# Softmax sums of a causal attention transposed and inverted once per query on VectorE, in a four-layer kernel with a hand-written order

## The reference

```python
x = L0(x)   # attention over 1024 tokens, query and key of width 32, x + gamma * out
x = L1(x)   # group norm, attention of width 256, output projection, x + out
x = L2(x)   # layer norms, 8 heads of width 32, causal, one key and value head, feed-forward
x = L3(x)   # as L1 with its own weights

# the part of L2 that the change touches
sim  = jnp.einsum('bhid,bjd->bhij', q, k)          # k, v shared by the 8 heads
sim  = jnp.where(causal, neg, sim)
attn = jax.nn.softmax(sim, axis=-1)                 # = exp(..) / sum of exp(..)
out  = jnp.einsum('bhij,bjd->bhid', attn, v)
out  = out.transpose(0, 2, 1, 3).reshape(b, n, INNER) @ wo
```

## Time and profile before

| | us |
|---|---|
| median of 3 runs | 1383.55 (1383.23 to 1387.08) |
| the profiled execution | 1385.56 |
| its span, first to last instruction | 1383.8 |
| PE busy | 1292.8 (93%) |
| DVE busy | 866.0 (63%) |
| ACT busy | 593.9 (43%) |
| POOL busy | 93.9 (7%) |
| mean granted clock of TensorE | 0.981 of full speed |

### The profile page before, as it was taken

How to read it: one execution, slowest core, us unless ns; L and a number is a source line. 1 busy time by engine, 2 the same in 40 slices (tenths; PEclk the granted TensorE clock), 3 DMA queues, 4 the chain that set the end, 5 groups by cost and what they waited for, 6 DMA issues and landing times.

```text
span 1383.8 us, 21791 instructions
## 1 busy us (share of the span) xinstructions
PE 1292.8 (93%) x8800; PEld 1011.3 (73%) x8800; DVE 866.0 (63%) x1854; ACT 593.9 (43%) x973; POOL 93.9 (7%) x134
## 2 busy tenths in 40 slices
PE   6979999889999999999999999999999999999898
PEld 5868777666678767677788667777787767768786
DVE  3634456787557587865567586776576768555451
ACT  3423343355444544444454344455325444443331
POOL 0000000110000000100100000000001000010000
PEclk9989999999999899999999999999999999999999
DMA  5000020110002010000020111000020100000000
GB/s 189 1 0 1 0 77 1 24 24 1 2 1 46 2 24 2 24 1 1 1 46 2 40 47 24 1 1 1 1 47 1 24 17 24 16 1 16 16 1 31
DMA packets 20611, 27.04 MB, mean 20 GB/s; under 512 B 3489, under 2 KB 14241, under 8 KB 20513
## 3 DMA queue, kind: packets, MB, share of 16 engines
q1 hardware_dynamic: 20512, 25.66, 6.7%
HBM read 8.61 MB, written 4.19 MB: 9 GB/s over the span
## 4 chain that ended last, share of the span: by engine, by line
PE 84%; DVE 8%; ACT 5%; issue 2%; DMA 0%; SPq 0%; POOL 0%; ACTq 0%; DVEq 0%
PE ring L728 28%; PE ring L781 25%; PE ring L1028 9%; PE ring L1009 5%; PE ring L992 5%; PE ring L772 5%; DVE part_max L1597 2%; ACT cprobs L1234 1%; PE ring L809 1%; PE ring L928 1%; PE ring L961 1%; PE ring L996 1%; ACT probs L1085 1%; PE ring L759 1%; DVE neg_max L1307 1%
## 5 line engine op out<-in xcount | busy, mean ns | idle before, releaser
L781 PE MATMUL ring<-probsT,vt 128*128 128x256 f32 x1536 | 361.7, 387 | 11.7 <-ACT probsT L1093 11.7
L781 PEld LDWEIGHTS ring<-probsT,vt 128*128 128x128 f32 x1536 | 290.4, 193 | 61.9 <-ACT probsT L1093 14.6
L1234 ACT ACTIVATE cprobs<-ring 128x1024 f32<-128x1024 f32 (+1 forms) x160 | 150.6, 941 | 206.1 <-PE ring L1009 205.7
L1085 ACT ACTIVATE probs<-ring,neg_max 128x1024 f32<-128x1024 f32 x96 | 107.0, 1115 | 200.3 <-DVE neg_max L1311 107.4
L1597 DVE TENSOR_REDUCE part_max<-ring 128x2 f32<-128x1024 f32 (+2 forms) x112 | 126.4, 1142 | 38.5 <-PE ring L992 24.0
L992 PE MATMUL ring<-ks,qs 96*128 96x512 f32 (+3 forms) x384 | 110.7, 385 | 15.1 <-ACT cprobs L1234 6.0
L1093 ACT COPY probsT<-ring 128x512 f32<-128x512 f32 x192 | 102.8, 591 | 26.2 <-PE ring L772 26.2
L1009 PE MATMUL ring<-qs,ks 98*128 98x512 f32 x288 | 107.5, 445 | 5.3 <-ACT probs L1085 2.5
L728 PE MATMUL ring<-h_hi,q_hi 128*128 128x512 f32 x256 | 107.4, 419 | 5.0 <-ACT cprobs L1234 2.8
L1310 DVE TENSOR_REDUCE shift_max<-ring 128x1 f32<-128x1024 f32 x64 | 78.2, 1222 | 53.2 <-PE ring L728 46.8
L772 PE MATMUL ring<-consts,probs 128*128 128x128 f32 x768 | 106.6, 280 | 5.0 <-ACT probs L1085 1.5
(11 more groups left out here) (221 smaller groups left out, 2128.2 us busy)
## 6 DMA issues: line engine op xcount, KB each, us to landing
qs<-q_hi SPq DMA_DIRECT2D x32, 128.0 KB, 2.3
qs<-q_hi SPq DMA_DIRECT2D x64, 64.0 KB, 2.0
x<-x_dram SPq DMA_DIRECT2D x3, 1024.0 KB, 6.5
qs<-q_lo SPq DMA_DIRECT2D x16, 128.0 KB, 2.3
qs<-max_rows SPq DMA_DIRECT2D x128, 2.0 KB
qs<-q_lo SPq DMA_DIRECT2D x32, 64.0 KB, 2.0
out_dram<-z SPq DMA_DIRECT2D x4, 512.0 KB, 2.8
out_dram<-x SPq DMA_DIRECT2D x4, 512.0 KB, 2.8
```

What stands on the lines that cost most here:

```text
L781: last = mm(o[:, ct * QUARTER:(ct + 1) * QUARTER], vt[:, j, ct * P:(ct + 1) * P], probsT[:, qi % (NQ - 1), j, :], start=j == 0, stop=j == ...
L1085: A(probs[:, ti % 2, :], flat(full_name(l, b, ("s", ti))), ACT.Exp, bias=neg_max[:, ti:ti + 1], accum_out=row_sum[:, ti:ti + 1]).then_inc( ...
L1234: A(causal_probs(step, n), heads(name)[:, :, 0:n], ACT.Exp).then_inc(read_done["c", "act"], 1)
```

## The change

`values` and its bank stay as they are. ACT no longer copies the two halves of the bank. DVE transposes the half with the sums in 32x32 squares straight from PSUM (`turned_sums`, 128x256), which puts the 32 queries of a square on partitions and makes the 32 columns of a square equal; it inverts one column of each of the 8 squares (128x8), reads that broadcast to 128x256 and transposes it back (`den`), and multiplies the other half of the bank, read from PSUM, by it. That product frees the bank, in place of ACT's copy. The cast and the subtraction stay. The three pieces of `normalise` are now: transposition; reciprocal and transposition back; product, cast and subtraction.

All five rows of `ORDER` are new. The number of pieces is the same on PE (1317, of which 664 full), on DVE (876), POOL and SP; ACT has 32 fewer. On PE the two chains alternate more often: 569 runs of one chain in the new row, 475 in the old one. The number of pieces between a block's final product and the piece that opens its bank again grows from 4 to 14 (mean of the 32 blocks).

```diff
@@ ORDER["PE"], first row @@
-        "0Fc4F60F2Fe50Fh234F60b3F560FFF1F734Fg017FFF2F45670FFF127FFF03F513F5F0246F012F405F710FFF2F456F012FFF3F5670b3F"
+        "0Fc4F60F2Fe50F72d5F401F760FFF3F516F021FFF3F0215ga1FFF027FFF03F513F5F0246F012F405F710FFF2F456F012FFF3F567a23F"
...
@@ -277,10 +277,22 @@
     for b, e in causal_order():
         if e[0] == "values":
             if is_final(e):
-                out.append((causal_name(b, e), "act", 1))
+                out.append((causal_name(b, e), "dve", 1))
         elif e[0] not in NO_UNIT:
             out.append((causal_name(b, e), "act" if e[0] in FILLED_BY_ACT else "dve", causal_banks(e)))
     return out
+
+
+def causal_reads():
+
+    units = {u[0]: u for u in causal_units()}
+    ends = [name for name in units if name.startswith("prep")]
+    for b, e in causal_order():
+        if e[0] == "norm" and e[2] == NORM_PIECES - 1:
+            ends.append(f"C{b}.o{e[1]}")
+        elif e[0] not in NO_UNIT and e[0] != "values":
+            ends.append(causal_name(b, e))
+    return [units[name] for name in ends]
 
 
 def queries(k, jt):
@@ -338,10 +350,10 @@
     place, previous = ring_places(ORDER["PE"])
     chain, freed_by, fill_no, rank = {}, {}, {}, {}
     for ch, us in units.items():
-        total = {"act": 0, "dve": 0}
         for i, (name, eng, _) in enumerate(us):
             chain[name], freed_by[name], fill_no[name] = ch, eng, i + 1
-        for name, eng, _ in full_units(False) if ch == "f" else us:
+        total = {"act": 0, "dve": 0}
+        for name, eng, _ in full_units(False) if ch == "f" else causal_reads():
             total[eng] += 1
             rank[name] = total[eng]
 
@@ -482,7 +494,9 @@
         gn_var, gn_rstd = sb("gn_var", [P, CT]), sb("gn_rstd", [P, CT])
         var_eps, rstd = sb("var_eps", [P, LN_SLOTS, 4]), sb("rstd", [P, LN_SLOTS, 4])
         ln_stats, ln_mv = sb("ln_stats", [P, LN_SLOTS, TPH, 6]), sb("ln_mv", [P, LN_SLOTS, TPH, 2])
-        sums = sb("sums", [P, 2, QUARTER])
+        turned_sums = sb("turned_sums", [P, TPH * 2, DH])
+        inverse = sb("inverse", [P, TPH * 2])
+        den = sb("den", [P, TPH * 2, DH])
         max_rows = sb("max_rows", [P, 2, QUARTER], F32R)
         part_max = sb("part_max", [P, TPQ, 2, 4])
         cmax = sb("cmax", [P, STACKS, TPQ, 4])
@@ -1232,16 +1246,6 @@
                         name = causal_name(b, e)
                         wait_filled(act, name)
                         A(causal_probs(step, n), heads(name)[:, :, 0:n], ACT.Exp).then_inc(read_done["c", "act"], 1)
-                    elif is_final(e):
-                        k = e[1]
-                        hg, qi = BLOCKS[k]
-                        wait_filled(act, causal_name(b, e))
-                        if b or k >= 2:
-                            act.wait_ge(out_ready, b * K + k - 1)
-                        acc = slot(causal_name(b, e))[:, 0, :]
-                        nc.scalar.copy(sums[:, k % 2, :], acc[:, QUARTER:])
-                        nc.scalar.copy(nums[:, hg, token_quarter(qi)],
-                                       acc[:, 0:QUARTER]).then_inc(read_done["c", "act"], 1)
                     elif len(e) == 2 and e[0] not in NO_UNIT + ("vt", "wo", "w1"):
                         stage(b, e)
                     else:
@@ -1611,16 +1615,19 @@
             def normalise(b, e):
                 _, k, piece = e
                 hg, qi = BLOCKS[k]
-                den = sums[:, k % 2, :]
+                name = f"C{b}.o{k}"
+                acc = slot(name)[:, 0, :]
                 if piece == 0:
-                    wait_read(dve, f"C{b}.o{k}")
-                if piece < 2:
-                    ins = v.reciprocal(den[:, piece * P:(piece + 1) * P], den[:, piece * P:(piece + 1) * P])
-                    if piece:
-                        causal_then(ins)
+                    wait_filled(dve, name)
+                    causal_then(v.transpose(turned_sums[:, :, :].rearrange("p s n -> p (s n)"), acc[:, QUARTER:]))
+                elif piece == 1:
+                    causal_then(v.reciprocal(inverse[:, :], turned_sums[:, :, 0]))
+                    causal_then(v.transpose(den[:, :, :], inverse[:, :].unsqueeze(2).broadcast_to([P, TPH * 2, DH])))
                 else:
                     to = token_quarter(qi)
-                    causal_then(v.tensor_tensor(nums[:, hg, to], nums[:, hg, to], den, ALU.mult))
+                    v.tensor_tensor(nums[:, hg, to], acc[:, 0:QUARTER], den[:, :, :].rearrange("p s n -> p (s n)"),
+                                    ALU.mult).then_inc(read_done["c", "dve"], 1)
+                    wait_read(dve, name)
                     causal_then(v.tensor_copy(heads_out[0][:, hg, to], nums[:, hg, to]))
                     v.tensor_tensor(heads_out[1][:, hg, to], nums[:, hg, to], f32(heads_out[0][:, hg, to]),
                                     ALU.subtract).then_inc(out_ready, 1)
```

More of the change, by code:

```diff
@@ L60 @@
[L60 to L70 removed]
+        "FFFFCFFFFFCCFFFCCFFFCCFFFFFFFFFFFFFFCCFFFFFFFFFFFFFFFFFFFFFFFFFFFFFFFFFFCFFFFFFCCFFFFFCCFFFFFFFFFCCFFFCCCCCF"
```

57 lines of the change are left out of this document (28 added, 29 removed).

## The result

The changed kernel takes 1399.47 us (median of 4 runs, 1398.32 to 1400.34); the kernel before took 1383.39 beside it. The ratio is 1.0112, 95% interval 1.0094 to 1.0130. The forecast was 1375 with a range to 1391, so the time moved the other way and lies above the range.

What follows compares the result with a forecast made beforehand. PE was taken as the bound, busy 1292.8 of 1383.8 us. Terms -2.5 - 8.3 - 3.5 - 2.9 - 1 + 7.6 + 1.5 = -9.1 us gave 1376.5, expected median 1374.5, written 1375; range 1365 to 1391.

Steps and rivals of the forecast that it cites:

- 35 to 45 us of idle time between 175 and 1290 us: Sign in the profile after: PE's idle time in the middle, down from 51.9 us; over 50 would favour the first rival.
- first rival: Middle gives nothing back: accumulators' banks are out of use 10 pieces longer; 1389, or 1395 with more waits; chance 0.23.
- more half-clock stretches: Sign against the forecast: PE's half-clock stretches grow in number, which no count of idle time foresees; no size given.
- The lighter DVE, -8.3: Middle, four thin stretches: DVE sheds 0.69 us a block, 12 us there, so PE idles 8.3 us less, by proportion.
- its clock, -3.5: Thin stretches: 26% of their 13.7 us clock loss goes, the same share as of their idle time.
- ACT's waits, -2.5: PE's three waits for `nums`, copied by ACT, disappear as 14 pieces instead of 4 precede the bank's reopening: -2.5 us.
- The bank, 0: DVE frees the accumulator's bank only at its third piece; costed at nothing, since 14 pieces, some 15 us, cover it.
- The rival of 1389 to 1395: The first rival: thin stretches short of banks, not DVE; 1389, or 1395 with 0.2 us more waits a block; chance 0.23.
- The head, -2.9 and -1: End of L0.0: L3's weight products move into PE's 2.86 us wait, saving 2.9 us, plus 1 us of clock.
- The tail, +7.6 and +1.5: Last feed-forward quarter, end of causal chain: PE idles 9.3 us instead of 1.74, costing 7.6, plus 1.5 of clock.
- The slow transposition: Rival: a transposition takes 1.86 us, adding 2.1 us of DVE a block; 1409 us, chance 0.04.

Runs made afterwards that it cites:

- `head_on_old`: Kernel before with inversion by transpositions, plus the new order's start on PE, ACT and DVE up to L1.0: 1383.00 us, ratio 0.9985.
- `tail_kept_warm`: Kernel after with 25 never-read products put ahead of the five waiting products of the last feed-forward quarter and last boundary: 1392.95 us, ratio 1.0075.
- `light_masks_elsewhere`: Kernel after with five causal maxima taken over 32 keys where PE is nearly full (598 to 612 us): 1397.82 us, ratio 1.0085.

## Why the prediction was wrong

**The step that failed is the one that is missing.** The prediction said that "the question is only where PE idles and who ends it", and then priced the new order at two places, both at the ends. Between them, where the order moves most of its pieces, it priced only the bank. Two layer boundaries (L1.2, L0.3) moved there from beside exponentials and products to beside the maxima of block 4; at the third place, in C3, a maximum waits for the bank of another. Taking the maxima's work away gives 11 us back in the new order and at most 2.6 in the old: that is the size of the missing term. With the tail's 10.6 it is more than the 18.2 us that the forecast let the operations and the head give. Whether other banks in the same order would have saved the 11 us was not tried.

The prediction's own signs did not settle it. It took 35 to 45 us of idle time between 175 and 1290 us for the forecast, and over 50 for its first rival. Measured are 55.6. It also named more half-clock stretches as a way to be wrong "which no count of idle time here foresees". They did not grow in number, but the one in the tail grew from 6.8 to 17.1 us.

**The lighter DVE, -8.3, and its clock, -3.5.** It was called the weakest number, and it was mis-sized: about -3 for both together in the old order (interval -5.5 to -0.6), and 0 in the new one with ACT's part included. The proportion read two kinds of stretches as if the one quantity that differed set the other. The two runs with light maxima show what is true of two places: 4.5 us less of DVE in a full stretch change nothing, and at the boundary most of it counts (3.2 us by equal work; by the medians 2.3 to 3.5, against the two measurements of the kernel after). A share of busy time over 70 to 175 us does not tell these apart. That 32.0 us of idle time remained in the thin stretches where I forecast less than before was right as a sign, but the idle time had only moved.

**ACT's waits, -2.5.** They are gone from the profile; what they were worth was not tried by itself.

**The bank, 0.** Right for the accumulator's own bank, as far as the runs tell. No wait of PE names `nums` or `den`, and the old operations, which free that bank at once, are no faster in the new order; a cost of a few us that their heavier DVE balances is not excluded. The rival of 1389 to 1395 ("a shortage of banks") was half right. The order keeps the accumulators' banks set aside longer whatever the operations, the maxima's are opened again sooner, and PE's waits for maxima are waits for banks. But what holds those banks is DVE, which has not yet read them, and the rival's price of 0.2 us a block says nothing of where.

**The head, -2.9 and -1.** The 2.86 us at 71 us are gone, but 2.47 us now stand at 56.46 us, ahead of an earlier group of the same products. By equal work the two kernels differ by -2.5 us at 108.7 us once the first product's start is taken off, and in the medians of `head_on_old` nothing is left.

**The tail, +7.6 and +1.5.** The mechanism was right and so were the four waits: 8.7 us against 9.3. The sum is 10.6 against 9.1, and the term that was too small is the clock: half clock lasts 17.1 us in place of 6.8. `tail_kept_warm` puts the whole of it at 3.8 us by equal work and 6.5 in the medians, against 1.5.

**The slow transposition.** Ruled out: 0.44 us, where 1.86 was feared.

In the middle the profile by equal work shows +5.9 us (-1.0 to +4.9), less than the 11 that the maxima cost. The rest would fit some 3 us that the operations give and a few that the order gains elsewhere; those were not separated. Nor was an order tried that keeps the new middle and moves the boundaries off the maxima.

## What to carry to other kernels

Where an order is new, list the boundaries of one chain (here a group norm: statistics, small product, root, coefficients, split) and read what the other chain has beside each, before and after. A boundary is covered only by work that does not need the same engine: the maxima beside the DVE-bound group norm of L1.2 covered nothing. Look also at which bank each piece opens there, and which engine has to read it first. A microsecond taken from DVE was worth most of one where PE stood and waited for it, and nothing in a full stretch, so a proportion between stretches should not carry the largest term of a sum. Where a wait can't be covered, work that nobody reads can keep PE's clock up. In the tail that was worth as much as covering it; at the group norm of L1.2 it gave 1 to 2 us.

## What the runs showed of the hardware that was not expected

A transposition of 128x256 float32 in 32x32 squares took the same from PSUM (443 ns) and from a source of 8 columns read broadcast (446 ns). A product with one operand in PSUM took 418 ns, no more than the 459 of both in SBUF.

The half clock lasted longer than the waits that it came with: five waits of 1.1 to 3.6 us, 12.3 us in all, ended between 1301 and 1319 us, and the clock stood at 1.2 GHz for 17.1 us from 1307.8. 25 products of 128x256 put into them, two instructions each (16 instructions took 3.70 us), kept it at 2.4 GHz throughout.

The executions of the kernel before spread over 1379.8 to 1389.6 us on the chips of this case, as much as most of the terms above. Differences under 3 us were therefore read from the profiled executions by equal work. Over a whole execution such a reading is weaker than the medians; at one place it is steadier: from 300 us to the end the difference between `light_masks_elsewhere` and the kernel after moves by 0.2 us only.
